# Attention rows stored from GpSimd's queue, x's columns normalised on VectorE

## The reference

```
x = x + attn(layernorm(x)) @ Wo        # q = elu(xn @ Wq) + 1, k = elu(xn @ Wk) + 1, v = xn @ Wv
                                       # a = sigmoid(xn @ Wa + ba + 2)
                                       # S = a*S + k^T v, z = a*z + k, out = (q S) / (q z + 1e-6), row by row
x = x + layernorm(x) @ CB.T * (SCB / 127) + bias
```

## Time and profile before

| | us |
|---|---|
| median of 3 runs | 1962.0 (1961.59 to 1962.97) |
| the profiled execution's own time | 1964.17 |
| its span, first to last instruction | 1962.4 |
| PE busy | 1939.8 (99%) |
| PEld busy | 1690.4 (86%) |
| DVE busy | 1645.8 (84%) |
| ACT busy | 687.0 (35%) |
| POOL busy | 392.9 (20%) |

### The profile page before, as it was taken

One profiled execution on the slowest core, in us unless ns is written; L12 is line 12 of the kernel. 1 busy time (PEld: TensorE's weight loads), 2 busy tenths in 40 slices (PEclk: granted clock), 3 DMA queues, 4 the chain that ended last, 5 costly groups with the idle time before them and its releaser, 6 DMA issues.

```text
span 1962.4 us, 69099 instructions
## 1 busy us (share of the span) xinstructions
PE 1939.8 (99%) x26926; PEld 1690.4 (86%) x26926; DVE 1645.8 (84%) x2918; ACT 687.0 (35%) x1288; POOL 392.9 (20%) x368
## 2 busy tenths in 40 slices
PE   8999999999999999999999999999999999999999
PEld 6888888898888988888889888888878888888887
DVE  8788888888888888888888888888787777777776
ACT  5333344333433343334333433334432222222221
POOL 3222222232222222332222223322010000000000
PEclk9999999999999999999999999999999999999999
DMA  6334444444444444444344444444477666666664
GB/s 216 89 93 97 98 111 100 109 104 104 104 97 98 102 109 100 107 106 108 95 98 100 113 95 109 106 111 124 91 165 175 161 161 161 160 161 161 160 161 117
DMA packets 596067, 237.40 MB, mean 121 GB/s; under 512 B 432064, under 2 KB 546240, under 8 KB 596032
## 3 DMA queue, kind: packets, MB, share of 16 engines
q1 hardware_dynamic: 560896, 204.94, 44.2%
q10 hardware_dynamic: 35136, 32.00, 5.7%
HBM read 168.59 MB, written 51.97 MB: 112 GB/s over the span
## 4 chain that ended last, share of the span: by engine, by line
PE 96%; DVE 2%; issue 1%; DMA 1%; SPq 0%; POOL 0%; POOLq 0%; ACT 0%; DVEq 0%
PE G L1332 54%; PE DS L1290 17%; PE NUM L1290 8%; PE NUM L1401 4%; PE SC L1454 3%; PE DS L1433 3%; PE NUM L1415 3%; PE SC L1280 2%; PE DS L1474 1%; DVE w_lo L917 0%; DMA norm_rows<-moments 0%; DVE w_lo L949 0%; DMA abc<-decay_rows 0%; DMA product_rows<-pT 0%; DVE D L1114 0%
## 5 line engine op out<-in xcount | busy, mean ns | idle before, releaser
L1332 PE MATMUL G<-w_hi,xT_hi 128*128 128x512 f32 x1024 | 406.9, 397 | 0.9 <-DVE w_lo L917 0.9
L1332 PE MATMUL G<-w_lo,xT_hi 128*128 128x512 f32 x1024 | 400.1, 391 | 0.0
L1332 PE MATMUL G<-w_hi,xT_lo 128*128 128x512 f32 x1024 | 398.7, 389 | 0.0
L738 ACT ACTIVATE relu_t<-G 128x512 f32<-128x512 f32 x256 | 153.1, 598 | 452.6 <-PE G L1332 450.4
L1332 PE MATMUL G<-xT_hi,w_hi 128*128 128x256 f32 x1024 | 290.2, 283 | 0.2 <-DVE w_lo L917 0.2
L1332 PE MATMUL G<-xT_lo,w_hi 128*128 128x256 f32 x1024 | 289.8, 283 | 0.0
L1332 PE MATMUL G<-xT_hi,w_lo 128*128 128x256 f32 x1024 | 289.7, 283 | 0.0
L1332 PEld LDWEIGHTS G<-w_hi,xT_hi 128*128 128x128 f32 x1024 | 192.4, 188 | 42.9 <-DVE xT_lo L910 1.0
L1332 PEld LDWEIGHTS G<-w_hi,xT_lo 128*128 128x128 f32 x1024 | 192.3, 188 | 41.4
L1332 PEld LDWEIGHTS G<-w_lo,xT_hi 128*128 128x128 f32 x1024 | 192.5, 188 | 35.5
L706 ACT ACTIVATE w_hi<-at_rows 128x512 fp32r<-128x512 f32 x128 | 73.9, 625 | 381.2 <-PE DS L1290 352.2
(11 more groups left out here) (137 smaller groups left out, 3609.2 us busy)
## 6 DMA issues: line engine op xcount, KB each, us to landing
abc<-decay_rows SPq DMA_DIRECT2D x256, 128.0 KB, 3.3
pbc<-product_rows SPq DMA_DIRECT2D x256, 128.0 KB, 3.1
attn_cols<-attn SPq DMA_DIRECT2D x512, 64.0 KB, 2.2
at_rows<-attn_cols ACTq DMA_DIRECT2D x244, 128.0 KB, 2.8
xt<-in_x SPq DMA_DIRECT2D x64, 256.0 KB, 3.2
x_in<-in_x SPq DMA_DIRECT2D x64, 256.0 KB, 3.0
out_rows<-xt SPq DMA_DIRECT2D x64, 256.0 KB, 3.0
xT_in<-in_xT SPq DMA_DIRECT2D x31, 512.0 KB, 4.4
```

The lines of the kernel that those rows point to most:

```text
L738: act.activation(relu_t[buffer][:, :], bank[:, :], ACT.Relu)
L1332: made = nc.tensor.matmul(to, lhs, rhs, start=(n == 0), stop=(n == len(passes) - 1))
```

## The change

- `store_rows` moves from SP's queue to GpSimd's, with the same four DMAs for each half and the same destinations. In a step GpSimd first does `inverse_deviation` (at b = 0), then stores half 1 of chunk i - 2, then half 0 of chunk i - 1.
- The two operations on x's columns move from GpSimd (8 instructions of 128x256 in a pair) to VectorE (2 instructions of 128x1024), put between the units of q in the step b = 0.
- ScalarE copies the table of the norm from `bias_b` into a new tile `norm_c`, in which the means of all 256 rows stand side by side, and the deviations too. VectorE reads that. The store of the table stays as it was.
- At the end of phase one the small power and the four scalings on GpSimd move from i = NC to i = NC + 1, behind the stores of i = NC.

```diff
-        norm_b = bias_b[:, :].rearrange("p (c s a) -> p a s c", s=2, a=2)
+        norm_c = sb("norm_c", [128, 4 * C])
+        norm_b = norm_c[:, :].rearrange("p (a s c) -> p a s c", s=2, a=2)
+        x_tiles = xT_in[:, :, :].rearrange("p k (s c) -> p k s c", s=2)
...
# sync, step
-                if exists(i - 2) and not (isinstance(i, int) and i == NC + 1):
-                    store_rows(1, i - 2, one[-2])
...
-                if exists(i - 1):
-                    store_rows(0, i - 1, one[-1])
# sync, step2
-                if isinstance(i, int) and i == 3:
-                    store_rows(1, NC - 1, NC)
# gpsimd
+            def store_rows(r, n, count):
...
+                pool.wait_ge(attn_ready[r], count)
+                for c in range(2):
+                    for half in range(2):
+                        q = 64 * c + SQ * half
+                        pool.dma_start(cols_of(here)[c, r, :, :, SQ * half:SQ * half + SQ],
+                                       attn[q:q + SQ, U * r:U * r + U].rearrange("f (b t) -> f b t", t=SQ))\
+                            .then_inc(attn_stored[r], 16)
+
             def step(i, pair, b):
+                one = counts(pool, i, 1, (-2, -1))
                 if b == 0 and exists(i + 2):
-                    pairs = counts(pool, pair, 1, (0, 1))
-                    p16 = counts(pool, pair, 16, (0,))
-                    inverse_deviation(pairs[1])
-                    x4 = xT_in[:, :, :].rearrange("p k (s c) -> p k s c", s=2)
-                    pool.wait_ge(xT_loaded, p16[0])
-                    pool.wait_ge(norm_loaded, p16[0])
-                    for kt in range(KT):
-                        made = pool.tensor_tensor(x4[:, kt, :, :], x4[:, kt, :, :], norm_b[:, 0, :, :], ALU.subtract)
-                    made.then_inc(xT_centred, 1)
-                    pool.wait_ge(xT_centred, pairs[0])
-                    for kt in range(KT):
-                        made = pool.tensor_tensor(x4[:, kt, :, :], x4[:, kt, :, :], norm_b[:, 1, :, :], ALU.mult)
-                    made.then_inc(xT_normal, 1)
-                if isinstance(i, int) and i == NC:
+                    inverse_deviation(counts(pool, pair, 1, (1,))[1])
+                if isinstance(i, int) and i == NC + 1:
                     inverse_deviation2(1)
+                if exists(i - 2) and not (isinstance(i, int) and i == NC + 1):
+                    store_rows(1, i - 2, one[-2])
+                if exists(i - 1):
+                    store_rows(0, i - 1, one[-1])
+                if isinstance(i, int) and i == NC + 1:
                     pool.wait_ge(wf_loaded, 16 * KT)
                     pool.wait_ge(scaled, 1)
                     for kt in range(KT):
...
             def step2(i, _, b):
                 if exists(i) and not (isinstance(i, int) and i == 1):
                     inverse_deviation2(counts(pool, i, 1, (0,))[0])
+                if isinstance(i, int) and i == 3:
+                    store_rows(1, NC - 1, NC)
# scalar, step
+                def norm_by_rows():
+
+                    act.wait_ge(norm_loaded, p16[0])
+                    wait(act, xT_normal, pairs[-1])
+                    act.activation(norm_b, bias_b[:, :].rearrange("p (c s a) -> p a s c", s=2, a=2), ACT.Copy)\
+                        .then_inc(norm_ready, 1)
...
                 elif exists(i):
+                    if exists(i + 2):
+                        norm_by_rows()
                     q_parts(2)
                     q_parts(3)
# vector, step
+                def over_tiles(a):
+
+                    return norm_b[:, a:a + 1, :, :].broadcast_to([128, KT, 2, C])
+
+                def centred_columns():
+
+                    dve.wait_ge(xT_loaded, x16[0])
+                    dve.wait_ge(norm_ready, pairs[0])
+                    nc.vector.tensor_tensor(x_tiles, x_tiles, over_tiles(0), ALU.subtract).then_inc(xT_centred, 1)
+
+                def normal_columns():
+
+                    dve.wait_ge(xT_centred, pairs[0])
+                    nc.vector.tensor_tensor(x_tiles, x_tiles, over_tiles(1), ALU.mult).then_inc(xT_normal, 1)
...
                 elif exists(i + 1):
+                    if exists(i + 2):
+                        centred_columns()
                     elu_q(2, 1)
                     decay_matrix(0)
+                    if exists(i + 2):
+                        normal_columns()
                     elu_q(3, 0)
```

More of the change, by code:

```diff
@@ L257, in gated_linear_attention_block @@
         norm_loaded = sem("norm_loaded")
+        norm_ready = sem("norm_ready")
         bias_loaded = sem("bias_loaded")
@@ L420, in ffn_weights @@
                     .then_inc(bias_loaded, 16)
[L422 to L431, removed]
             def load_x(n, b):
@@ L635, in inverse_deviation2 @@
                 pool.tensor_tensor(rstd2[:, :], vareps2[:, :], minus_half[:, 0:1], ALU.pow).then_inc(rstd2_ready, 1)
+            def store_rows(r, n, count):
+                here = n
+                if not isinstance(n, int):
+                    here = pool.snap(n)
+                    pool.compute_val(here)
+                pool.wait_ge(attn_ready[r], count)
[5 more added lines that the diff above has]
+                            .then_inc(attn_stored[r], 16)
             def step(i, pair, b):
+                one = counts(pool, i, 1, (-2, -1))
                 if b == 0 and exists(i + 2):
-                    pairs = counts(pool, pair, 1, (0, 1))
-                    p16 = counts(pool, pair, 16, (0,))
-                    inverse_deviation(pairs[1])
-                    x4 = xT_in[:, :, :].rearrange("p k (s c) -> p k s c", s=2)
-                    pool.wait_ge(xT_loaded, p16[0])
-                    pool.wait_ge(norm_loaded, p16[0])
-                    for kt in range(KT):
-                        made = pool.tensor_tensor(x4[:, kt, :, :], x4[:, kt, :, :], norm_b[:, 0, :, :], ALU.subtract)
-                    made.then_inc(xT_centred, 1)
-                    pool.wait_ge(xT_centred, pairs[0])
-                    for kt in range(KT):
-                        made = pool.tensor_tensor(x4[:, kt, :, :], x4[:, kt, :, :], norm_b[:, 1, :, :], ALU.mult)
-                    made.then_inc(xT_normal, 1)
-                if isinstance(i, int) and i == NC:
-                    inverse_deviation2(1)
+                    inverse_deviation(counts(pool, pair, 1, (1,))[1])
+                if isinstance(i, int) and i == NC + 1:
+                    inverse_deviation2(1)
+                if exists(i - 2) and not (isinstance(i, int) and i == NC + 1):
[3 more added lines that the diff above has]
+                if isinstance(i, int) and i == NC + 1:
                     pool.wait_ge(wf_loaded, 16 * KT)
@@ L709, in step @@
                 one = counts(act, i, 1, (-3, -2, -1, 0, 1))
-                pairs = counts(act, pair, 1, (0, 1))
+                pairs = counts(act, pair, 1, (-1, 0, 1))
+                p16 = counts(act, pair, 16, (0,))
                 c32 = counts(act, i, 32, (0, 1))
```

## The result

| | before | after |
|---|---|---|
| median, us (runs beside each other on one chip) | 1962.49 (1961.59 to 1963.13) | 1978.71 (1977.95 to 1979.01) |
| span of the profiled execution | 1962.4 | 1977.1 |

The kernel became slower: ratio 1.0081, 95% interval 1.0068 to 1.0093, or +16.2 us. The forecast was 1966.5 with a range from 1960.5 to 1977, so the direction was right and the size was outside the range. Executions of one kernel differ by some 2 to 3 us either way, and the profiled one of the kernel before lay 1.7 us above its median.

The account below looks back on a forecast made before the run. TensorE, busy for 1939.8 of 1962.4 us, was taken as the bound. The start's -0.8 and the end of phase one's +5.3, with nothing in the loop, gave +4.5 us: median 1966.5, range 1960.5 to 1977.

Parts of the forecast that it names:

- SP's queue: In the loop, eight issues a step leave SP, so loads and the norm's store go out earlier; gain nothing.
- So the loop hides them: GpSimd's eight store issues a step, 10.4 us of 21.9, fit in the loop before the norm's table is needed; no cost.
- (d): Rival: GpSimd's issues slow VectorE and TensorE loses at hand-overs of the loop, at most 0.3 us a pair; 1975; chance 0.04.
- Any wait of TensorE inside the loop: Sign that the forecast is wrong; the forecast expected a pair still of 43.80 us.
- One GpSimd issue, t: Time of one store's issue on GpSimd: taken as 1.3 us, between 0.63 and 2.5.
- (b): Rival: the 512 pieces cost, t of 1.7 to 2.7 us, +7.7 to +15.7 us, at 2.5 1976.1; chance 0.17.
- (c): Rival: GpSimd bounds the loop, t above 2.74 us; at 3.0 +130 us, about 2095; chance 0.08.
- (a): Rival: not slower, GpSimd's issue as short as SP's, t below 0.9 us; 1961.2, up to 1963.3; chance 0.20.
- The turn: End of phase one: eight store issues ahead of the first small power make it 6.4 us late; +5.3 us, or 8t - 5.1.
- The start: TensorE's 2.2 us wait for `elu_k` shrinks as VectorE's queue is no longer slowed by GpSimd; -0.8 us, bounds 0 and 2.2.
- VectorE's new work and what it gets back: Two new instructions at 1.24 us each against 1.8 us or more given back a pair; load changes by less than +1 us.
- ScalarE's copy: One instruction of 512 columns, some 0.6 us, in ScalarE's idle gap before the relu of q's unit 2; cost nothing.

Follow-up runs that it names:

- e3: The kernel after, but in each step b = 1 GpSimd waits for the next chunk's products to land before storing half 0; 1966.31 us, ratio 1.0022 to the kernel before.
- e2: The kernel before with only the stores moved to GpSimd's queue, the norm's work still on GpSimd; 1984.49 us, ratio 1.012 to the kernel before.
- e4: The kernel after, with GpSimd's two small powers and four scalings ahead of the stores at the end of phase one; 1977.70 us, ratio 1.0089 to the kernel before.
- e7: e3 with the last twelve stores issued by SP and GpSimd's first power and scalings where they stood before; 1960.55 and 1960.83 us, ratio 0.9989 to the kernel before.
- e1: The kernel after with all stores back in SP's queue, so only the norm's work is moved; 1960.92 us, ratio 0.9994 to the kernel before.
- e8: The kernel after, but SP issues one group of four stores (half 0 of chunk 59) four steps ahead of the turn; 1975.16 us in one run.
- e6: e1, but in odd steps SP issues the four stores of half 0 directly ahead of the loads of products; 2036.80 us, ratio 1.0364 to the kernel before.

## Why the prediction was wrong

**The step that failed** is "SP's queue": "TensorE has no wait on a DMA in the earlier trace rows, so this gives nothing", and its twin, "So the loop hides them". I counted the time of GpSimd's eight issues and asked whether GpSimd had room for it. I didn't ask what the transfers would run beside. TensorE indeed waited for no DMA, but ScalarE did, one step ahead of the copy of kT: its row was in the trace of before (20.0 us, 29 times) and I never put it beside the order of SP's queue, in which the stores stood behind those loads. The cost was 12.0 us (e3, e2). None of my rivals named it; (d), "TensorE loses at tight hand-overs of the loop", came near the time (1975) with the wrong cause. Of "loads of decays and products and the norm's store go out earlier" only the norm's store came true in the pair above (733.05 against 733.79 + 1.5); the stores of half 0 had stood behind the loads. "Any wait of TensorE inside the loop" was among the marks of a wrong prediction, and that is what came.

**One GpSimd issue, t.** I took 1.3 us, with 0.63 to 2.5 as bounds. It is 0.62 us in the median, SP's own time and my lower end:

```profile
L633 POOL DMA_DIRECT2D attn_cols<-attn x512: 620/622/807, 62.1 to 1481.0; - x171
```

The row nearest to it was the issue of the same DMA by another engine; I leaned towards GpSimd's arithmetic, which is another kind of work. Rivals (b) and (c) fall with this ((c)'s 2095 also leaves out its own term for the turn: at t = 3.0 the sum is 1962 + 130 + 18.9 - 0.8, about 2110), and (a), the Trainium skill's side, was right on the price.

**The turn.** +5.3 forecast, +5.8 measured, which is luck. By my formula in t, 0.62 gives nothing, and the whole sum with it is -0.8: that the direction came out right is luck too. Instead 3.49 us came from the pause ahead of GpSimd's 508th store, which happens to be the eighth at the turn, and the rest from what followed it: VectorE's `residual_normal` at 2.71 us beside the scalings, and the lower clock behind TensorE's idle time. The place (the eight stores ahead of the power, the wait of VectorE behind it) was the right one, as e4 and e7 show.

**The start.** -0.8 forecast, -3.0 measured; the wait fell from 2.2 to 1.0 as told, yet the third copy of kT came 3.0 earlier. e1 has it and e2 doesn't, so it is the norm's move. I had priced one wait of TensorE. 1.5 us are there at the second copy of kT; the other 1.5 are the granted clock of 0.62 in 48 to 56 in the profiled execution of before, which no term of mine held and which isn't there in every execution.

**VectorE's new work and what it gets back.** Right. 1.22 and 1.20 us each against 1.24; `elu_q` at most 695 ns and `elu_k` 693, and the decay matrix at 1201 in the mean against 1365:

```profile
L1135 DVE TENSOR_TENSOR_SCAN D<-abc,eye 128x512 f32<-128x512 f32 x128 | 153.7, 1201 | 1.1 <-DMA abc<-decay_rows 1.1
```

**ScalarE's copy** takes 1.15 us, not 0.6. It reads with the 16-byte stride of the norm's table and writes side by side; that the stride makes the difference wasn't tried apart. It cost nothing, as e1 shows. "Nothing" was right, the size was not.

The sum in the right sizes: -3.0 + 12.0 + 5.8 gives the +14.7 of the spans (the parts are rounded), where I had -0.8 + 0 + 5.3. The medians differ by 16.2, for the profiled execution of before was 1.7 us above its median and that of after 0.1.

## What to carry to other kernels

Moving a DMA to another queue moves its bytes in time, and the order within one queue was protecting whatever stood ahead of it: before pricing the issue, list the loads that will be in flight beside it, and follow each to its first waiter, even where that waiter is not the bound. An engine's wait on a load (here ScalarE's, 0.7 us a time) with little slack behind it is the row to look for, one hop upstream of the engine that bounds. If a store must go by a second queue, let it wait for the landing of the load that matters; that was two lines here and gave back 12 us. And a difference of 1 or 2 us between two single profiles is read only beside the granted clock of the same stretch.

## What the hardware showed that I had not expected

- Of two 128 KB loads the second landed in the median 3.2 to 3.4 us after its issue with 64 KB stores of the same queue ahead of or behind it, 4.8 us beside those of GpSimd's queue and 4.2 beside those of ScalarE's.
- A store of 512 pieces of 128 bytes costs GpSimd's queue 0.62 us to issue, the same as SP's, and lands after 3.1 us in the median rather than 2.2.
- GpSimd pauses ahead of every 28th DMA that it issues, 0.8 us in the loop; at the 508th it was 2.3 to 3.7 us in six kernels, and 0.23 in e8, where four issues fewer had moved it behind the turn.
- After TensorE's wait of 4.9 us at the turn its granted clock was 0.57 over 8 us, and in e6, behind a wait of 2.4 us in the loop, 0.79 over 8 us.
- ScalarE's copy of 512 columns with a 16-byte stride in its input took 1.15 us, its copies side by side 0.60.
